# A new slot table for a chunk pipeline: wider gaps between the steps, scatters spread into the next iteration

## The reference

```
# tokens: 5 shifted copies of a 2-channel 104x104 image, normed, 8x8 patches -> 169 tokens of 128
h = conv(layernorm(shifts(x)) * gamma + beta, W) + b              # (16, 169, 128)
h = concat([h, txt], axis=1)                                      # (16, 681, 128)
# mixing over time
z = layernorm(h)
y = p_t * cumsum(p_s * z, axis=1)                                 # p_s, p_t: powers of a decay per channel
h = h + y @ mix_w.T + mix_b
# mixture of 8 experts, 2 per token
xf = layernorm(h)
topw, topi = top_k(xf @ Wg, 2);  topw = softmax(topw)
out = h + sum over the 2 experts e of topw_e * ((silu(xf @ Wg_e + bg) * (xf @ Wu_e + bu)) @ Wd_e + bd_e)
```

## Time and profile before

| what | value |
|---|---|
| median of 3 runs | 821.02 us (817.80 to 824.27) |
| profiled execution | 824.18 us, its span 822.4 us |
| PE busy | 603.9 us (73%), mean granted clock 0.835 |
| PE weight load | 519.1 us (63%) |
| POOL busy | 498.1 us (61%), 520 instructions |
| DVE busy | 430.1 us (52%) |
| ACT busy | 264.7 us (32%) |
| DMA | 125.23 MB, 152 GB/s on average |

### The profile page before, as it was taken

One profiled execution on the slowest core, in us unless ns is written; L12 is line 12 of the kernel. 1 busy time (PEld: TensorE's weight loads), 2 busy tenths in 40 slices (PEclk: granted clock), 3 DMA queues, 4 the chain that ended last, 5 costly groups with the idle time before them and its releaser, 6 DMA issues.

```text
span 822.4 us, 12791 instructions
## 1 busy us (share of the span) xinstructions
PE 603.9 (73%) x3335; PEld 519.1 (63%) x3335; DVE 430.1 (52%) x1708; ACT 264.7 (32%) x690; POOL 498.1 (61%) x520
## 2 busy tenths in 40 slices
PE   3787645327778788698989986999898969999000
PEld 2687634316567576586878875888787758888000
DVE  4789655343556657265655766355544623445122
ACT  2502122112234432244442543254253324444000
POOL 5602327763655756377677776477777767760674
PEclk9998855557789988698997997899999979999555
DMA  7185000126345533565655663667577768984221
GB/s 152 53 290 148 1 0 26 33 90 186 101 127 153 145 104 106 164 194 150 185 169 154 205 198 106 191 202 218 179 214 235 236 197 257 279 279 147 80 77 61
DMA packets 84597, 125.23 MB, mean 152 GB/s; under 512 B 15044, under 2 KB 57792, under 8 KB 84526
## 3 DMA queue, kind: packets, MB, share of 16 engines
q1 hardware_dynamic: 72526, 101.66, 40.9%
q0 software_dynamic: 11520, 22.35, 9.5%
q10 hardware_dynamic: 480, 0.41, 0.4%
HBM read 84.25 MB, written 43.25 MB: 155 GB/s over the span
## 4 chain that ended last, share of the span: by engine, by line
PE 37%; POOL 21%; DVE 14%; issue 13%; DMA 7%; ACT 3%; SPq 3%; POOLq 0%; DVEq 0%; ACTq 0%
PE gu L587 15%; PE dn L587 11%; POOL gat L1048 8%; POOL xbuf L1034 8%; PE mx L587 5%; POOL rs L966 3%; DMA gat<-ybuf,ypos 3%; PE xTp L765 3%; DMA space<-xbuf 2%; DMA space<-in_x_dram 2%; PE tr L587 2%; ACT x L894 1%; PE tr L719 1%; DVE gat L1485 1%; DVE rec L1268 1%
## 5 line engine op out<-in xcount | busy, mean ns | idle before, releaser
L1034 POOL DMA_INDIRECT xbuf<-x,pos x180 | 186.4, 1035 | 112.9 <-DVE pos L1369 56.0
L587 PE MATMUL gu<-space,wts 128*128 128x256 f32 x912 | 246.0, 410 | 9.1 <-DVE space L1476 9.1
L1476 DVE SCALAR_TENSOR_TENSOR space<-gu,wts,space 128x256 f32<-128x256 f32 x228 | 109.1, 482 | 235.7 <-ACT space L912 173.3
L1048 POOL DMA_INDIRECT gat<-ybuf,ypos x180 | 177.7, 987 | 87.9 <-issue 55.5
L912 ACT ACTIVATE space<-gu,wts 128x256 f32<-128x256 f32 x228 | 109.1, 479 | 305.7 <-PE gu L587 305.3
L587 PEld LDWEIGHTS gu<-space,wts 128*128 128x128 f32 x912 | 174.8, 206 | 32.0 <-DVE space L1476 10.9
L587 PEld LDWEIGHTS dn<-wts,space 128*128 128x128 f32 x912 | 127.9, 204 | 14.1 <-DVE space L1476 7.1
L587 PE MATMUL dn<-wts,space 128*128 128x128 f32 x912 | 129.1, 288 | 5.8 <-DVE space L1476 5.8
L765 PE MATMUL xTp<-cst,space 128*128 128x128 f32 x228 | 51.8, 311 | 40.2 <-DMA space<-xbuf 38.1
L765 PEld LDWEIGHTS xTp<-cst,space 128*128 128x128 f32 x228 | 26.7, 154 | 52.6 <-DMA space<-xbuf 40.8
L966 POOL TENSOR_TENSOR rs<-ve,nhalf 128x4 f32<-128x4 f32 (+2 forms) x39 | 40.4, 1036 | 29.7 <-DVE ve L1281 15.2
(11 more groups left out here) (198 smaller groups left out, 837.8 us busy)
## 6 DMA issues: line engine op xcount, KB each, us to landing
wts<-wall SPq DMA_DIRECT2D x114, 386.0 KB
space<-xbuf SPq DMA_DIRECT2D x114, 128.0 KB, 2.6
ybuf<-space SPq DMA_DIRECT2D x114, 128.0 KB
xbuf<-zero_rows SPq DMA_DIRECT2D x4, 1024.0 KB, 10.5
xt<-in_txt_dram SPq DMA_DIRECT2D x16, 256.0 KB, 3.0
xbuf<-zero_rows SPq DMA_DIRECT2D x32, 128.0 KB
out_dram<-gat SPq DMA_DIRECT2D x16, 256.0 KB
xbuf<-x,pos POOLq DMA_INDIRECT x180
```

The source lines that it names most:

```text
L587: return nc.tensor.matmul(o, l, r, start=a, stop=z_)
L1034: nc.gpsimd.indirect_dma_start(out=xbuf, out_offset=bass.IndirectOffsetOnAxis(pos[0:p, c:c + 1], 0), in_=x2[n % NX2][0:p, m // 2 * D:(m // ...
L1048: nc.gpsimd.indirect_dma_start(out=gat[b][0:p, (k * W4 + j) * D:(k * W4 + j + 1) * D], out_offset=None, in_=ybuf[g], in_offset=bass.Indire ...
L1476: V.scalar_tensor_tensor(hid[q % 4], gu_ps[q % 3][:, SLOT:2 * SLOT], wts[k % NW][:, W_B + HT + t:W_B + HT + t + 1], sil[q % 3], ALU.add, A ...
```

## The change

Every step gets another place in the table, so that between a step and the one that feeds it on another engine lie two to five slots, and up to twelve from `routing` to `rank`. `rank`, `place` and `weights` move from slots 1 to 3 to slots 10 to 13 of their iteration. The scatters no longer have fixed slots 3 to 13 of their own iteration: the eight of a chunk stand on every second slot from slot 15 on, so seven of them lie in the next iteration; only those of a group's last chunk stand on consecutive slots. The first unit of each group moves from slot 1 to slot 9 (positions 73, 185, 297, 377), and units and gathers move with it, in unchanged number and spacing. The tile table moves from slot 4 to slot 13, the padding from slot 6 to 15, the places of the results from slot 10 to slot 6 of the next iteration. Waits that were written with fixed offsets are now derived by `latest`. One more buffer holds the normed chunk (`NX2` 4).

```diff
-FIRST = -4
-ITERS = 30
-AT = dict(text_load=(5, 8), text_stats=(4, 3), text_var=(4, 4), norm1=(4, 5), z_norm=(4, 14),
...
+FIRST = -3
+ITERS = 34
+AT = dict(text_load=(4, 2), text_stats=(3, 0), text_var=(3, 1), norm1=(3, 4), z_norm=(3, 8), z_T=(3, 13), text_decay=(3, 15),
...
-SCATTER_SLOTS = (3, 4, 6, 7, 8, 11, 12, 13)
-TABLE_SLOT, PAD_SLOT, RESULT_SLOT = 4, 6, 10
+TABLE_SLOT, PAD_SLOT, RESULT_SLOT = 13, 15, 6
...
+def latest(step, other, n):
+
+    at = (n - AT[other][0]) * SLOTS + AT[other][1]
+    m = AT[step][0] + (at - 1 - AT[step][1]) // SLOTS
+    return max(min(m, CHUNKS - 1), IMG_CHUNKS - 1 if step in TEXT_STEPS else -1)
...
-TILE_FROM = [b * SLOTS + 1 for a, b in GROUPS]
+TILE_FROM = [b * SLOTS + 9 for a, b in GROUPS]
...
-NX2 = 3
+NX2 = 4
...
+SCATTERS_AT = by_slot([(n * SLOTS + 15 + m * (1 if (n + 1) in [b for a, b in GROUPS] else 2), (n, m))
+                       for n in range(CHUNKS) for m in range(2 * width(n))])
...
-                m = n - AT["mix"][0]
+                m = latest("rank", "mix", n)
...
-                    if s in SCATTER_SLOTS and 0 <= i < CHUNKS:
-                        scatter(i, SCATTER_SLOTS.index(s))
+                    for n, m in scatters(i, s):
+                        scatter(n, m)
...
-                        if s == RESULT_SLOT and i == GROUPS[g][1] - 1:
+                        if s == RESULT_SLOT and i == GROUPS[g][1]:
```

More of the change, by code:

```diff
@@ L113 @@
 SLOTS = 16
-FIRST = -4
-ITERS = 30
-AT = dict(text_load=(5, 8), text_stats=(4, 3), text_var=(4, 4), norm1=(4, 5), z_norm=(4, 14),
-          z_T=(3, 11), text_decay=(3, 12), text_sums=(3, 13), text_y=(2, 0),
-          mix=(2, 5), mixed=(2, 6), mixed_stats=(2, 7), mixed_var=(2, 8), norm2=(2, 9), x_norm=(2, 12),
-          x_T=(1, 2), x_keep=(1, 3), logits=(1, 6), keep_logits=(1, 9), top_value=(1, 11), top_index=(1, 14),
-          gate_exp=(1, 15), routing=(1, 15), rank=(0, 1), place=(0, 2), weights=(0, 3))
+FIRST = -3
+ITERS = 34
+AT = dict(text_load=(4, 2), text_stats=(3, 0), text_var=(3, 1), norm1=(3, 4), z_norm=(3, 8), z_T=(3, 13), text_decay=(3, 15),
+          text_sums=(2, 0), text_y=(2, 2), mix=(2, 4), mixed=(2, 7), mixed_stats=(2, 8), mixed_var=(2, 9), norm2=(2, 12),
+          x_norm=(1, 0), x_T=(1, 4), x_keep=(1, 6), logits=(1, 9), keep_logits=(1, 11), top_value=(1, 12),
+          top_index=(1, 13), routing=(1, 14), gate_exp=(0, 2), rank=(0, 10), place=(0, 12), weights=(0, 13))
 TEXT_STEPS = ("text_load", "text_stats", "text_var", "norm1", "z_norm", "z_T", "text_decay", "text_sums", "text_y")
-SCATTER_SLOTS = (3, 4, 6, 7, 8, 11, 12, 13)
-TABLE_SLOT, PAD_SLOT, RESULT_SLOT = 4, 6, 10
+TABLE_SLOT, PAD_SLOT, RESULT_SLOT = 13, 15, 6
 def due(step, i, s):
@@ L188, in gathers, with scatters @@
     return GATHERS_AT.get(i * SLOTS + s, [])
+def scatters(i, s):
+    return SCATTERS_AT.get(i * SLOTS + s, [])
 def combines(i, s):
@@ L714, in x_T @@
                 wait(pe, W.kept_ok, n)
-                before = n - AT["x_T"][0] + AT["z_T"][0] - 1
-                if before >= IMG_CHUNKS:
-                    pe.wait_ge(W.zs_ok, min(before, CHUNKS - 1) - IMG_CHUNKS + 1)
+                wait(pe, W.zs_ok, latest("z_T", "x_T", n) - IMG_CHUNKS + 1)
                 for j in range(width(n)):
@@ L724, in z_T @@
                 pe.wait_ge(W.z_ok, b + 1)
-                m = n - AT["z_T"][0] + AT["x_T"][0]
-                pe.wait_ge(W.kept_ok, m + 1)
+                wait(pe, W.kept_ok, latest("logits", "z_T", n) + 1)
                 for j in range(W4):
@@ L743, in ranks @@
                 pe.wait_ge(W.mask_ok, n + 1)
-                pe.wait_ge(W.h1_ok, min(n + AT["mix"][0], CHUNKS))
+                wait(pe, W.h1_ok, latest("mix", "rank", n) + 1)
                 ones = ones_r[0:p, 0:p]
@@ L1027, in scatter @@
                 p, w = parts(n), width(n)
-                if m >= 2 * w:
-                    return
                 if m == 0:
```

## The result

The changed kernel takes **835.5 us** (median of 4 runs, 833.49 to 836.19), against 820.66 us for the kernel before on the same chip. The ratio is 1.0174, 95% interval 1.013 to 1.0219: slower, by 1.3 to 2.2%. The forecast was 811.0 us with a range of 797 to 829. The rival on the other side, the late scan at 831 us with a chance of 18%, came nearest.

What follows compares the result with a forecast made beforehand. POOL was taken to bound groups 1 and 2, latency group 0. Opening +4.1, group 0 -12.5, group 1 +1.2 and group 2 -2.8 gave -10.0 us: 811.0 us on the median of 821.02, range 797 to 829.

Steps and rivals of the forecast that it cites:

- the late scan: Rival, 18%: `text_y` holds POOL's stream while DVE is in its row; group 0's five periods grow to 21 us; 831 us.
- The opening: Before the first tile: `rank` of chunk 0 stands behind later steps, first scatter at 134.1 instead of 127.4; +4.1 us.
- the period of group 0's run: Chunks 5 to 9 beside group 0's tiles: 17.3 us each, helping the run take 122.9 instead of 137.4 us.
- The chain: Group 0's longest cycle: `text_y`, `mix`, a tile, `logits`, `rank`, DVE's row ending in the scan; sum 17.8, taken as 17.3 us.
- The first period of group 0: Chunk 4, the first in group 0's run: 16.5 us.
- The wait for `mask`: PE's 19.8 us of waits for `mask` in group 0 would go, since twelve slots lie between `routing` and `rank`.
- The starts: First scatter after the first tile of groups 0, 1 and 2: later by 2.0, 3.0 and 3.9 us.
- Group 1: Stage of group 1: POOL was the bound and stays it; sum +1.2 us.
- Group 2: Stage of group 2, POOL-bound with PE close: fewer waits and one norm less against a later start; sum -2.8 us.
- POOL's pace everywhere: Rival, 22%: the chain has slack, group 0's run goes at POOL's 16.3 us a chunk; 801 us.
- The norm blocks `place`: Rival, 5%: `norm2` sharing slot 12 with `place` costs 1 us in five periods; 816 us.
- The rule of the Trainium skill: DVE instructions with two SBUF inputs and GpSimd ones reading SBUF exclude each other; `spot` could wait 1 us a period, charged nothing.

Runs made afterwards that it cites:

- the seventh experiment: The kernel before with `text_y` at (2, 4) instead of (2, 0), behind the chunk's first scatters on POOL: 850.19 us, ratio 1.0376.
- the fifth experiment: The kernel before with each group's first unit at slot 3 instead of 1, behind `rank` and `place` of the next group's first chunk: 809.39 us, ratio 0.9882.
- the two repairs: The changed kernel with `text_decay` and `text_sums` ahead of `top_index` and `routing`, and each group's first unit at slot 13 instead of 9: 800.13 us, ratio 0.9725.
- the tenth experiment: The changed kernel with four added matmuls per text chunk, result overwritten, behind PE's wait for `yT`: 831.64 us, ratio 1.0133.

## Why the prediction was wrong

**The opening: right.** The first scatter came at 134.99 (134.1 forecast) and the first tile at 192.06 (191 forecast), +4.8 against +4.1.

**The step that failed: "I take 17.3, nearer to the lower end", the period of group 0's run.** The chain was the right one, down to its last link. Its links on PE were priced from rows at full clock, `mix` at 2.4 us with its bias row and the tile at 4.0, from the earlier trace rows. In the turn shown they took 2.9 and 5.9 us, because the wait for `yT` was followed by matmuls at the lower clock. These 2.4 us are nearly all of the 2.6 by which that turn exceeds 17.3. Five periods were put at 17.3 and measured 19.8 on average, +12.5 us. The run with the added matmuls ahead of the wait, where the clock was 0.86 and not 0.78, measured 17.3. The prediction had named 19.6 us as the other end for this period, and had leaned away from it because DVE is busy 62% of the window; a busy share says nothing of how long a ring of waits takes. In this ring a link that waited was followed by a slower one, and so a turn grew by more than its wait. The clock of 0.86 in the earlier trace rows had been read as a fact of that stage and not as a price that a new wait could raise.

**The first period of group 0** was put at 16.5 and took 21.3 us, +4.8. After two scatters POOL stood 4.9 us in `text_y` for the scan. The prediction charged this only to the last chunk, where it was nearly right (18.8 us measured, 19.9 forecast, -1.1). With the 1.4 us of a later start and -0.3 at the end, that gives the 17.4 us by which the stage missed.

**The wait for `mask`** went away as said, and so did its price. It had been worth little: in the kernel before, filling 6 us of it left the stage at 148.9 us against 149.2, and without the long `mask` rows, in the seventh experiment, the stage was no shorter.

**The starts** were priced at 2.0, 3.0 and 3.9 us and cost 3.4, 4.0 and 5.1: right in kind, 3.6 us too low together. They should have been asked the other way too: the fifth experiment shows 12 us to be had in the kernel before by leaving the tile until the ranking is done.

**Group 1** (+4.1 against +1.2): the start took 1.0 us more than forecast and the run 2.3. PE waited 11.8 us for `yT` there as well, five times, so POOL was not its bound throughout. **Group 2** (-5.0 against -2.8): the run took 130.0 us, 2.6 less than forecast. POOL as the bound was right there, at a clock of 0.99.

**Of the rivals**, the late scan named the mechanism: POOL's stream held by `text_y` while DVE is in its row. Its period of 21 us stands beside 19.8 measured over the same five, past its turning point of 19.3. Its reason was not the right one: hiddens of DVE do stand in that row (the one of 279.24 just ahead of `rank`), but from `logits` to the scan the turn is as long at the full clock as here (8.4 us in both). What grew were `mix` and the tile ahead of them. It had 18% because the feeding distance of two slots was counted for what it says in slots, and not for what a wait on it does to PE. "POOL's pace everywhere" was reached by no version: with the two repairs the five periods of group 0 averaged 17.2 us, where it wanted 16.3. "The norm blocks `place`" can be ruled out as a cost: the slowest `spot` in the tiles of the changed kernel took 0.27 us.

**The rule of the Trainium skill** was weighed rightly for `rs` and too lightly for `text_y`. In the kernel before every `mask`, `hit` or `spot` of over 0.5 us ends 0.05 to 0.1 us behind the end of a `text_y` (six rows, 0.94 to 2.67 us); with `text_y` moved away from them in the seventh experiment none took over 0.26 us. In the row of 209.56 the wait began while POOL was still in a scatter and `ex`, 1.4 us ahead of `text_y`; why is open. "SBUF — State Buffer", section "Who interferes with whom", gives the rule of exclusion: the trace agrees for the GpSimd instruction with two 128x512 inputs, and not for those of 128x4.

What remains open: 5.7 of the 14.8 us between the medians, which the two profiled executions don't show, and why the clock was higher in the tenth experiment although PE waited as long.

## What to carry to other kernels

Follow the ring, not the wait: before moving a step, write down the cycle of steps that feed one another across the engines, and price it once with TensorE at the full clock and once with the part behind every wait of TensorE at the half clock; if the two lie on either side of the present period, the change can go either way. Put the step whose result closes the ring first in its engine's row, ahead of small steps with slack, since POOL's and PE's streams stand behind it in order. And where a group's last steps and the next group's first compete, let the step that another engine's stream waits for go first. Here that was the ranking, which lets POOL scatter, ahead of the tile: 12 to 13 us in either kernel.

## What the runs showed of the hardware

- Two short pauses of TensorE, 1.33 us before 259.74 and 0.77 us before 267.08, were followed by close to 7 us at 1.2 GHz that began in the middle of full work, between 267.1 and 269.3. They nearly doubled the `gu` of the tile (3.62 us instead of 1.89). With the second pause filled, the first alone (1.33 us before 258.79) left the clock at 1.00. With both pauses left and four matmuls more behind the second (the tenth experiment) it stayed at 1.00 as well, so the pauses are not the whole condition.
- Work that nobody reads made a kernel faster: 28 added matmuls in group 0, 8.1 us of busy time, shortened its stage by 10.5 us and the whole from a ratio of 1.0174 to 1.0011. Placed behind the wait they shortened the stage by 6.6 us in the profiled execution, while the whole (1.0133) can't be told from the kernel without them.
- DVE's `mask`, an addition of two SBUF inputs (104x32), took 2.67 us where it met POOL's multiply of 128x512 (it began 1.4 us ahead of that multiply and ended 0.05 us behind it), against 0.19 us elsewhere; inside POOL's `ex` of 128x4 at 252, and inside an `rs` at 134, it took 0.19 us.
